# Two-layer transformer with routed experts: first layer's experts fetch rows through a table made by one-hot products

## What is computed

```python
for _ in range(LOOPS):                       # 2
    zn = _rmsnorm(z, norm_w)
    x = zn.reshape(T, D)                     # T = 4096, D = 256
    combine = _combine_weights(x, w_macro, w_micro)
    h = jax.nn.silu(jnp.einsum('td,efd->tef', x, w1))    # e: 8 experts, f: 512
    y = jnp.einsum('tef,edf->ted', h, w2)
    mixed = jnp.einsum('ted,te->td', y, combine)
    z = z + mixed.reshape(B, S, D)
```

## Time and profile before

| | |
|---|---|
| median of 3 runs | 3723.95 us (3721.77 to 3724.22) |
| profiled execution, its own time | 3725.22 us |
| its span in the profile | 3723.4 us |
| TensorE busy | 2677.6 us (72%) |
| VectorE busy | 2024.0 us (54%) |
| ScalarE busy | 1581.2 us (42%) |
| GpSimd busy | 1075.6 us (29%) |
| first layer's rms_logits, route, experts and combine_qkv | from 1119.8 to 2310.5 us |

### The profile page before, as it was taken

One profiled execution on the slowest core, in us unless ns is written; L12 is line 12 of the kernel. 1 busy time (PEld: TensorE's weight loads), 2 busy tenths in 40 slices (PEclk: granted clock), 3 DMA queues, 4 the chain that ended last, 5 costly groups with the idle time before them and its releaser, 6 DMA issues. The chain is left out here.

```text
span 3723.4 us, 63993 instructions
## 1 busy us (share of the span) xinstructions
PE 2677.6 (72%) x15884; PEld 1588.9 (43%) x15885; DVE 2024.0 (54%) x4912; ACT 1581.2 (42%) x2482; POOL 1075.6 (29%) x1687
## 2 busy tenths in 40 slices
PE   8699999999764089904099766788888877178870
PEld 5333333333244078804088633444444445044440
DVE  3588888888453534434134365667676735544205
ACT  3377777777543034411044322466666644011112
POOL 1211111111060600060600175222221124377637
PEclk9699999999965589955599988899999976588985
DMA  6200110010135222230222266111111021022312
GB/s 164 49 18 17 23 23 17 17 23 17 38 106 201 78 75 73 67 95 8 97 71 73 87 159 161 27 23 23 29 29 23 18 67 36 31 78 80 98 36 90
DMA packets 394873, 227.69 MB, mean 61 GB/s; under 512 B 291774, under 2 KB 380594, under 8 KB 393859
## 3 DMA queue, kind: packets, MB, share of 16 engines
q1 hardware_dynamic: 239380, 132.04, 12.6%
q10 hardware_dynamic: 129280, 52.45, 4.9%
q0 software_dynamic: 26112, 42.09, 3.7%
HBM read 135.66 MB, written 128.97 MB: 71 GB/s over the span
## 5 line engine op out<-in xcount | busy, mean ns | idle before, releaser
L317 ACT ACTIVATE att_pr<-att_S 128x1024 f32<-128x1024 f32 (+1 forms) x896 | 835.9, 941 | 429.6 <-ACTq L324 426.7
L357 DVE TENSOR_REDUCE att_mparts<-att_S 128x2 f32<-128x1024 f32 x640 | 776.9, 1224 | 171.8 <-DVEq L353 167.4
L233 PE MATMUL att_S<-att_qT,att_kT 64*128 64x512 f32 (+3 forms) x1792 | 430.4, 473 | 44.8 <-PEq L228 41.1
L249 PE MATMUL att_OP<-att_pr,att_vn 128*32 128x512 f32 (+3 forms) x3584 | 452.8, 565 | 1.0 <-PEq L243 0.7
L221 PE MATMUL att_S<-att_kT,att_qT 64*128 64x512 f32 (+3 forms) x1792 | 391.9, 432 | 74.9 <-PEq L215 65.1
L233 PEld LDWEIGHTS att_S<-att_qT,att_kT 64*128 64x128 f32 x1792 | 174.8, 184 | 470.5 <-issue 459.4
L169 POOL COPY att_vn<-att_raw 128x256 f32<-128x256 f32 x64 | 25.4, 398 | 1151.5 <-POOLq L168 1151.5
L1299 POOL DMA_INDIRECT sorted_in<-l_norm,ffn_target x256 | 254.7, 995 | 155.2 <-issue 84.9
L363 DVE CUSTOM_DVE_ANT_0 att_unused<-att_S,att_mask 128x128 f32<-128x128 f32 (+3 forms) x512 | 228.4, 488 | 73.1 <-DVEq L353 73.0
L221 PEld LDWEIGHTS att_S<-att_kT,att_qT 64*128 64x128 f32 x1792 | 188.1, 191 | 174.7 <-issue 170.0
L1020 PE MATMUL experts_TX<-experts_ident,experts_xs 128*128 128x128 f32 x288 | 56.3, 278 | 211.0 <-PEq L1018 210.8
(11 more groups left out here) (280 smaller groups left out, 5041.3 us busy)
## 6 DMA issues: line engine op xcount, KB each, us to landing
qkv<-qkv_y ACTq DMA_DIRECT2D x64, 384.0 KB, 3.3
att_raw<-qkv SPq DMA_DIRECT2D x96, 256.0 KB, 3.2
experts_xs<-sorted_in SPq DMA_DIRECT2D x144, 128.0 KB, 2.0
sorted_out<-experts_y ACTq DMA_DIRECT2D x144, 128.0 KB
ffn_w<-in_w SPq DMA_DIRECT2D x16, 1024.0 KB
ao<-att_aon SPq DMA_DIRECT2D x32, 256.0 KB, 2.4
post_at<-ao SPq DMA_DIRECT2D x64, 128.0 KB, 2.8
ffn_w<-in_w SPq DMA_DIRECT2D x2, 4096.0 KB
```

Of the source, the lines that this page charges most:

```text
L233: mm=pe.matmul(S[:,b,h,f:512],kT[r,s,kt*128:kt*128+128],qT[r,s,c*512+f:c*512+512],start=True,stop=not diag)
L249: mm=pe.matmul(OP[32*j:32*j+32,f:512],vn[:,s,kt,h,:],pr[:,n%4,h,f:512],start=kt<2,stop=g in last_groups,skip_group_check=True)
L317: nc.scalar.activation(pr[:,n%4,:,f:512],S[:,ring["e",n],:,f:512],ACT.Exp,scale=exp_scale).then_inc(s_free[ring["e",n]],1)
L357: nc.vector.tensor_reduce(mparts[:,s,:,2*qt+half],S[:,b,:,0:width(qt,half)],AX.X,ALU.max).then_inc(end,1)
```

## The change

**rms_logits** also stores the scaled rows to a DRAM tensor scaled (SP, keep). The zero fill goes. In the second pass the two rows of each token are loaded from a DRAM tensor mixed, where they lie in token order, with one plain DMA of 128x2x256 a tile on SP.

**route** no longer keeps slot. From each pair's place it makes the slot's number and the row in it. For 8 of the 64 columns of pairs at a time (CHUNKS = 8) VectorE compares them with a row of numbers: in_slot 128x8x72 and in_row 128x8x128, both bf16 with ones where they agree. GpSimd multiplies in_slot by the number of the column and by the number of the token in its tile, and TensorE adds 64 products of 128x128 by 128x144 in IX. The result, at row p and slot t, names the pair whose place that is. From it come source (the token to fetch) and target (the row of mixed to write; for empty places beyond the tensor). In the first pass the split of the weights stands here: high parts on ScalarE, remainders on GpSimd, ahead of GpSimd's work on the table.

**experts** has no first part. GpSimd gathers xs from scaled by source and scatters y to mixed by target; places beyond the tensor are skipped. y has four buffers.

**combine_qkv** loads the rows from mixed with plain DMAs on SP (eight buffers), and GpSimd keeps the roots alone.

The diff, cut:

```diff
+def both_rows(ap,b,u):
+    return ap.rearrange("(s n) c -> n s c",s=2)[bass.ds(b*SEQ+u*128,128)]
@@ rms_logits
+        ZR=8; zs=m.sb("zs",[128,ZR,DIM]); zT=m.sb("zT",[128,2,DIM])
...
-                    for i in range(SLOTS0*128//chunk):
-                        sp.dma_start(xs_d[i*chunk:(i+1)*chunk].rearrange("(p b) c -> p (b c)",p=128),zeros_d).then_inc(prepared,16)
...
+                if combined:
+                    def load(b,u):
+                        sp.wait_ge(rows_free,1).then_inc(rows_free,-1)
+                        sp.dma_start(rows[:,u%R],both_rows(y2_d,b,u)).then_inc(rows_loaded[u%R],16)
+                    pipelined(sp,[load])
+                def keep(b,u):
+                    sp.wait_ge(zs_keep,1).then_inc(zs_keep,-1)
+                    sp.dma_start(rows_of(zs_d,b,u),zs[:,u%ZR]).then_inc(zs_kept[u%ZR],16)
+                pipelined(sp,[keep])
+                if prepare: sp.wait_ge(prepared,32)
...
-                                nc.gpsimd.indirect_dma_start(out=rows[:,n%R,s,:],out_offset=None,in_=ys_d,in_offset=bass.IndirectOffsetOnAxis(ap=slot[:,s,n:n+1],axis=0)).then_inc(rows_loaded[n%R],16)
@@ route
+                for low,high in parts:
+                    pool.wait_ge(high_ready,1).then_inc(high_ready,-1)
+                    nc.gpsimd.tensor_tensor(low,low.bitcast(F32),high.bitcast(F32),ALU.subtract).then_inc(low_done,1)
+                for c in range(CHUNKS):
+                    pool.wait_ge(hot_ready,1).then_inc(hot_ready,-1)
+                    qs=place[:,PER_CHUNK*c:PER_CHUNK*c+PER_CHUNK].rearrange("p (q o) -> p q o",o=1).broadcast_to([128,PER_CHUNK,SLOTS0])
+                    nc.gpsimd.tensor_tensor(named[:,c%2,:,0,:],in_slot[:,c%2],qs,ALU.mult).then_inc(pool_done,1)
+                    nc.gpsimd.tensor_scalar(named[:,c%2,:,1,:],in_slot[:,c%2],marks[:,128+Q:128+Q+1],None,ALU.mult).then_inc(pool_done,1)
+                    pool.wait_ge(pool_done,2).then_inc(pool_done,-2)
+                    pool.sem_inc(named_ready,1)
...
+                for low,high in parts: nc.scalar.activation(high,low.bitcast(F32),ACT.Copy).then_inc(high_ready,1)
...
+                for c in range(CHUNKS):
+                    pe.wait_ge(named_ready,1).then_inc(named_ready,-1)
+                    for i in range(PER_CHUNK):
+                        mm=pe.matmul(IX[:].rearrange("p a j -> p (a j)"),in_row[:,c%2,i,:],named[:,c%2,i].rearrange("p a j -> p (a j)"),start=c==0 and i==0,stop=c==CHUNKS-1 and i==PER_CHUNK-1)
+                    mm.then_inc(hot_free if c<CHUNKS-1 else table_full,1)
...
+                dve.sem_inc(hot_free,2)
+                def hot(c):
+                    dve.wait_ge(hot_free,1).then_inc(hot_free,-1)
+                    for out,at,n in ((in_slot,slotb,SLOTS0),(in_row,rowb,128)):
+                        all_=iota[:,0:n].rearrange("p (o n) -> p o n",o=1).broadcast_to([128,PER_CHUNK,n])
+                        this=at[:,PER_CHUNK*c:PER_CHUNK*c+PER_CHUNK].rearrange("p (q o) -> p q o",o=1).broadcast_to([128,PER_CHUNK,n])
+                        V.tensor_tensor(out[:,c%2],all_,this,ALU.is_equal).then_inc(dve_done,1)
+                    dve.wait_ge(dve_done,2).then_inc(dve_done,-2)
+                    dve.sem_inc(hot_ready,1)
+                for n in range(CHUNKS): hot(n)
...
+                dve.wait_ge(table_full,1).then_inc(table_full,-1)
+                ts(number[:],IX[:,0,:],128.0,-128.0,ALU.mult,ALU.add)
+                tt(number[:],number[:],IX[:,1,:],ALU.add)
+                done(V.tensor_copy(numberi[:],number[:]))
+                ts(source[:].bitcast(I32),numberi[:],TOK-1,None,ALU.bitwise_and)
+                ts(target[:].bitcast(I32),numberi[:],4*TOK-1,None,ALU.bitwise_and)
@@ experts
-                for t in range(NT):
-                    pool.wait_ge(zn_ready,1).then_inc(zn_ready,-1)
-                    for s in range(2):
-                        nc.gpsimd.indirect_dma_start(out=xs_d,out_offset=bass.IndirectOffsetOnAxis(ap=slot[:,s,t:t+1],axis=0),in_=zn[:,t%R,:],in_offset=None).then_inc(scattered[t%R],16)
...
+                BEHIND=4
+                def gather(t):
+                    pool.wait_ge(x_free,1).then_inc(x_free,-1)
+                    nc.gpsimd.indirect_dma_start(out=xs[:,t%R,:],out_offset=None,in_=zs_d,in_offset=bass.IndirectOffsetOnAxis(ap=source[:,t:t+1],axis=0)).then_inc(x_loaded[t%R],16)
+                def arrived(t):
+                    pool.wait_ge(x_loaded[t%R],16*(t//R+1))
+                    pool.sem_inc(x_arrived,1)
+                def scatter(t):
+                    pool.wait_ge(y_ready,1).then_inc(y_ready,-1)
+                    nc.gpsimd.indirect_dma_start(out=y2_d,out_offset=bass.IndirectOffsetOnAxis(ap=target[:,t:t+1],axis=0),in_=y[:,t%RY,:],in_offset=None,
+                                                 bounds_check=2*TOK-1,oob_is_err=False).then_inc(y_stored[t%RY],16)
+                def stored(t):
+                    pool.wait_ge(y_stored[t%RY],16*(t//RY+1))
+                    pool.sem_inc(y_kept,1)
+                for n in range(SLOTS0+BEHIND+1):
+                    for lag,stage in ((BEHIND+1,stored),(1,arrived),(0,gather),(BEHIND,scatter)):
+                        if 0<=n-lag<SLOTS0: stage(n-lag)
@@ combine_qkv
+                    sp.wait_ge(rows_free,1).then_inc(rows_free,-1)
+                    sp.dma_start(rows[:,u%RR],both_rows(y2_d,b,u)).then_inc(rows_loaded[u%RR],16)
...
-                for n in range(NT+7):
-                    for lag,stage in ((0,gather),(2,arrived),(3,root_z),(6,root_x)):
+                for n in range(NT+3):
+                    for lag,stage in ((0,root_z),(3,root_x)):
```

More of the change, by code:

```diff
@@ L835, in _ @@
                 pipelined(dve,[scaled,None,None,batch_out])
+                for i in range(ZR): dve.wait_ge(zs_kept[i],16)
             @block.tensor
@@ L852, in _, with route @@
                 pipelined(pe,[turn,product])
-def route(nc,tag,lg,tri_d,key_d,jv_d,slot,weight,eid):
+def route(nc,tag,lg,tri_d,key_d,jv_d,marks_d,weight,eid,source,target,split=None):
     with Mem(nc,tag) as m:
@@ L1067, in silu, with four @@
                     nc.scalar.activation(h[:,u%2],H[:,u%2,:],ACT.Silu).then_inc(h_ready,1)
-                def store(t,u):
-                    act.wait_ge(y_ready,1).then_inc(y_ready,-1)
-                    act.dma_start(ys_d[bass.ds(t*128,128),:],y[:,u%2]).then_inc(y_stored[u%2],16)
-                def four(t,last,first=False):
+                def four(last):
                     for u in range(U):
@@ L1075, in four @@
                         if not(last and u+1>=U): silu(u+1)
-                        if not(first and u==0): store(t+u-1,u-1)
                 x_high(0); x_high(1); silu(0)
-                four(0,False,first=True)
-                with act.Fori(1,SLOTS0//U-1) as j:
-                    four(j*U,False)
-                four(SLOTS0-U,True)
-                store(SLOTS0-1,U-1)
+                with act.Fori(0,SLOTS0//U-1):
+                    four(False)
+                four(True)
             @block.vector
@@ L1125, in _, with combine_qkv @@
                 four(True)
-                for i in range(2): dve.wait_ge(y_stored[i],16)
-def combine_qkv(nc,tag,z,slot,weight,ys_d,src,w_d,bias_d,x_out,qkv,ident_d):
+def combine_qkv(nc,tag,z,weight,y2_d,src,w_d,bias_d,x_out,qkv,ident_d):
     W=3*DIM
@@ L1160, in _ @@
                 pool.wait_ge(half_done,1)
-                def gather(n):
-                    if n>=R: pool.wait_ge(rows_free,1).then_inc(rows_free,-1)
-                    for s in range(2):
-                        nc.gpsimd.indirect_dma_start(out=rows[:,n%R,s,:],out_offset=None,in_=ys_d,in_offset=bass.IndirectOffsetOnAxis(ap=slot[:,s,n:n+1],axis=0)).then_inc(rows_loaded[n%R],16)
-                def arrived(n):
-                    pool.wait_ge(rows_loaded[n%R],32*(n//R+1))
-                    pool.sem_inc(rows_ready,1)
                 def root_z(n):
```

144 lines of the change are left out of this document (68 added, 76 removed).

## The result

The changed kernel takes 3779.2 us (median of 4 runs, 3778.5 to 3782.9), the kernel before 3724.1 (4 runs beside it): a ratio of 1.0149, with a 95% interval of 1.0132 to 1.0167. It is slower by 55 us. The forecast was 3718 us, a range of 3655 to 3775 and 0.47 for faster: direction and range both missed, mainly by one term.

The account below looks back on a forecast made before the run. GpSimd's scatters and gathers were taken to leave TensorE idle in the experts and the second rms_logits, with routing a VectorE chain. Terms -37 - 32 + 68 + 39 - 29 - 16 = -7 took 3725.2 to 3718 us, range 3655 to 3775.

Parts of the forecast that it names:

- The price of a serial round trip: Both experts' stages: each slot pays scatter landing, GpSimd wake and gather, so GpSimd sets the pace; -37 and -32 us.
- arrived(n-1) is never the last to wait: Experts, GpSimd's queue: a gather lands within 2.8 us of its start, so the wait for it never sets the pace.
- 2.4 + 0.65 + 1.3 = 4.35 us: Experts, time of a slot: scatter landing, GpSimd's wake, then gather with its gap, against 3.74 us before.
- The start and the end: Experts' stage: first scatter 19.6 us in, and 17 us after the 67 periods for last matmuls, stores and landing.
- Rival E: Experts: gather and scatter delay each other in one queue, landing 2.85 us, 4.8 us a slot; 3778 us, chance 0.10.
- Route, first pass: Weight subtractions and table on GpSimd hinder VectorE's chain; routing ends at 1291 instead of 1223, +68 us.
- exclusion with turns: First route: VectorE and GpSimd exclude each other; VectorE gets one two-input instruction between two subtractions, 2.6 us a turn.
- rival D: First route: VectorE gets no turn between subtractions of 2.94 us; +86 instead of +68, 3736 us, chance 0.19.
- Rival B: Routing: no exclusion to speak of between VectorE and GpSimd; +33 and +26 us, 3670 us in all, chance 0.20.
- Route, second pass: No split; positions 2.4 us later, table chunks of 4.6 us make 36.8, plus 3.5, less 3.3 hidden: +39 us.
- rms_logits: Second pass: plain loads replace 64 gathers, issue and landing set 1.6 us a step; 58 us against 87.4, -29.
- combine_qkv: GpSimd loses its gathers, so a tile takes 4.55 us instead of 5.01; -16 us, bounds -5 and -20.

Follow-up runs that it names:

- e1: Changed kernel with GpSimd's wait for a scatter in the experts one iteration later (slot n-6 instead of n-5): 3636.5 us, ratio 0.9763 to the kernel before.
- e2: Changed kernel with the order of GpSimd's two waits in the experts exchanged, the gather's ahead of the scatter's: 3765.7 us, ratio 1.0112 to the kernel before.
- e1b: Changed kernel with both GpSimd waits in the experts, for scatter and for gather, a whole iteration later: 3605.8 us, ratio 0.9686 to the kernel before.
- e4: Changed kernel without GpSimd's 16 subtractions in the first route: 3752.9 us, ratio 1.0078 to the kernel before.
- e5: Changed kernel with the first route's 16 subtractions made by VectorE within its own chain: ratio 1.0100 to the kernel before, first route 102.6 us.
- e6: Changed kernel with the table's product with one input moved from GpSimd to ScalarE: ratio 1.0071 to the kernel before, routes 97.9 and 70.3 us.
- e7: Changed kernel with the table's products off GpSimd, one on ScalarE and one on VectorE: ratio 1.0063 to the kernel before, routes 98.8 and 71.5 us.
- e11: Changed kernel with eight buffers instead of four for the second rms_logits' rows: ratio 1.0090 to the kernel before, rms_logits 106.2 us.

## Why the prediction was wrong, and where it was right

**The price of a serial round trip.** The mechanism stands: e1 and e2 show that the wait for the scatter issued just before made the slot, and that "arrived(n-1) is never the last to wait". The step that failed is the size of the term "2.4 + 0.65 + 1.3 = 4.35 us". It measured 2.47 + 1.00 + 1.28 = 4.75, so most of the error, 0.35 of 0.40 us, lies in the wake of GpSimd. The 0.65 us came from the earlier trace rows, a GpSimd that had one wait, for its own memset, in front of a transfer; here three semaphore instructions stood in the queue between the landing and the gather (0.2 us by their times), and the start behind the last of them took 0.8. Why 0.8 and not 0.65, no run shows. The landing was taken at the median "since it is also the minimum", and grew by 0.07. 0.4 us look small beside a bound of 5.45; times 72 slots and two passes they are 58 us, eight times the margin of 7 us on which the forecast of "faster" stood.

**The start and the end.** 0.6 and 5.9 us in the first pass. The 17 us of the end left too little for what the rows show there: four more scatters (16.6), a landing (2.2) and 4.1 us to the next stage.

**Rival E** had the number, 4.8 us a slot and 3778 us, and the wrong reason: it made the landing 2.85 us by gathers and scatters in one queue. The landing is 2.5, and e1b issues more transfers in the same time. That its number fits is luck. Had its chance been put on the size of the trip instead of on one mechanism, it would have had more than 0.10.

**Route, first pass** (+68, measured +66): right, and for its reason, exclusion with turns, which e4, e5, e6 and e7 show from four sides. Within it two errors partly cancelled: a turn took 2.35 us and not 2.6, and two of the 16 turns went to instructions with one input, which the forecast took to be free. Turns between two subtractions, and not the starving of rival D: the reserve of 2.94 us for a subtraction was not needed, 2.35 was measured. The trace agrees with the rule of the Trainium skill (SBUF — State Buffer, Who interferes with whom) where the earlier trace rows could show it only for short instructions: with a GpSimd subtraction of 2.35 us running, a VectorE tensor_tensor of 0.29 takes up to 2.46. Rival B is out.

**Route, second pass** (+39, measured +38.8): the sum is right, its parts less so. The product with one input takes 2.3 to 3.4 us and not 0.65, the other 1.15 and not 1.4, and VectorE's pair lies beside the longer one in part; the chunk came to 4.3 instead of 4.6 by two errors against each other.

**rms_logits** (-29, measured -30): the right size for a wrong reason. The forecast had the loads bound the step at 1.6 us; it is VectorE's own chain at 1.45 (e11).

**combine_qkv** (-16, measured -18.9): within its bounds of -5 and -20; no run tests the reason.

**The chances.** The sum of seven terms between -37 and +68 was -7. Its own range of 3690 to 3750 was too narrow for two terms of 67 periods each, with 0.45 us of doubt in a period: that alone is 60 us, and the measured time lay 29 us above it.

## What to carry to other kernels

Where one queue issues transfers and also waits for them, a wait should not be for the transfer issued just before it: one iteration of distance for the scatters' wait was worth 143 us here, one for the gathers' 31 more, at the price of no buffer. A helper engine's work beside the busy one is only hidden if the two don't exclude each other: work that went from GpSimd to ScalarE, or even in series onto VectorE, made the routing shorter. And a per-iteration cost that is multiplied by 144 must be known to 0.05 us (7 us in all) before a sum of a few microseconds says anything of the sign.

## What was not expected of the hardware

- From the last semaphore in its queue to the start of an indirect gather GpSimd takes 0.8 us here, with one more pair of wait and signal costing about 0.1 (e2).
- A VectorE tensor_scalar with one input waits for a GpSimd subtraction as one with two inputs does (2.13 us for 0.23), while reductions and reciprocals beside it keep their time (a reciprocal of 128x128 takes 0.95 us in both kernels).
- On GpSimd a multiplication by a column of values (one SBUF tile of 576 bf16 as input) is slower than the one of two tiles. The last chunk has both with little beside them, VectorE busy with a comparison until 1281.86 and then with a reduction:

```profile
1281.19 1.67 POOL L902 TENSOR_TENSOR route_named<-route_in_slot,route_place 128x576 bf16<-128x576 bf16 x1 [0.43 <-POOLq L900]
1282.84 1.72 POOL L903 TENSOR_SCALAR route_named<-route_in_slot,route_marks 128x576 bf16<-128x576 bf16 x1
```

The first is 1.15 us elsewhere and waited for VectorE; the second is at its shortest, 1.72 us. ScalarE makes the same product in 0.78 us.

- The same program's experts' stages took 278 and 275 us in one run and 297 and 296 in another, with TensorE's transposes handed to ScalarE in 0.40 and 0.78 us. A pace found in one set of runs need not hold in the next.
